# A graph-attention kernel: six PSUM banks a head that overlap the next head's, two matmuls for every i-tile, masks of -1

## What is computed

```python
seq = (x @ W_seq).reshape(N, H, DH)                  # N = 2048, H = 16, DH = 32
scores = leaky_relu(score1[:, :, None] + score2[:, None, :], 0.2)   # per head, (H, N, N)
attn = softmax(scores + (1 - adj) * -65500, axis=-1)
hidden = einsum('hij,jhd->ihd', attn, seq).reshape(N, 512)
x1 = layernorm(x + elu(hidden @ W_out + b_out))
A = D^-1/2 ((adj + adj.T) / 2 + I) D^-1/2            # second layer, same adj
out = layernorm(x1 + (adj @ A) @ x1)
```

## Time and profile before

| | us |
|---|---|
| median of 3 runs (lowest, highest) | 741.42 (740.29, 742.1) |
| profiled execution | 740.72 |
| its span, first to last instruction | 738.9 |

### The profile page before, as it was taken

One profiled execution on the slowest core, in us unless ns is written; L12 is line 12 of the kernel. 1 busy time (PEld: TensorE's weight loads), 2 busy tenths in 40 slices (PEclk: granted clock), 3 DMA queues, 4 the chain that ended last, 5 costly groups with the idle time before them and its releaser, 6 DMA issues.

```text
span 738.9 us, 23474 instructions
## 1 busy us (share of the span) xinstructions
PE 722.7 (98%) x10731; PEld 560.0 (76%) x10731; DVE 526.6 (71%) x885; ACT 409.6 (55%) x315; POOL 117.6 (16%) x145
## 2 busy tenths in 40 slices
PE   7999899999999999999999999999999999999996
PEld 5878899999999999999999995444444444444444
DVE  4568999999999999999999984877830110332332
ACT  1678998888988998898988952333220110000000
POOL 0200110001221212213000002655312100000000
PEclk9999999999999999999999999999999999999999
DMA  9994315213532344333221122994059500101101
GB/s 334 417 419 162 110 54 149 61 46 74 88 63 64 61 82 83 63 65 59 59 59 36 47 82 50 184 188 101 23 87 170 85 1 1 41 31 43 43 29 43
DMA packets 33351, 71.24 MB, mean 96 GB/s; under 512 B 3044, under 2 KB 14052, under 8 KB 31076
## 3 DMA queue, kind: packets, MB, share of 16 engines
q1 hardware_dynamic: 24736, 51.64, 20.3%
q0 software_dynamic: 8240, 17.84, 17.0%
q10 hardware_dynamic: 276, 0.26, 0.1%
HBM read 77.86 MB, written 8.65 MB: 117 GB/s over the span
## 4 chain that ended last, share of the span: by engine, by line
PE 81%; DVE 8%; issue 5%; DMA 4%; SPq 1%; POOL 1%; ACT 0%; POOLq 0%; DVEq 0%; ACTq 0%
PE bank L635 20%; PE bank L742 14%; PE bank L636 12%; PE bank L728 11%; PE bank L691 8%; PE bank L641 4%; PE bank L699 4%; PE bank L640 4%; PE bank L639 4%; DVE RZ L1081 3%; DMA RZ<-in_L_gnn_W_seq_dram 2%; DVE RG L1095 1%; DMA RZ<-s_rows_dram 1%; DVE RG L1091 1%; SPq L345 1%
## 5 line engine op out<-in xcount | busy, mean ns | idle before, releaser
L635 PE MATMUL bank<-RP,RG 128*128 128x132 f16 (+1 forms) x3072 | 375.3, 220 | 2.8 <-DVE RG L1091 1.5
L636 PE MATMUL bank<-RP,MT 128*128 128x66 f16 (+1 forms) x3072 | 375.0, 196 | 0.0
L820 ACT ACTIVATE RZ<-RZ,TAB 128x2048 int8<-128x2048 f32 x159 | 305.0, 1994 | 24.8 <-DVE RG L1091 22.1
L635 PEld LDWEIGHTS bank<-RP,RG 128*128 128x128 fp8e4 x3072 | 284.8, 98 | 3.7 <-DVE RG L1091 1.8
L636 PEld LDWEIGHTS bank<-RP,MT 128*128 128x128 fp8e4 x3072 | 284.7, 97 | 0.0
L640 PE MATMUL bank<-RP,RG 128*128 128x66 f16 (+1 forms) x1024 | 199.2, 194 | 0.0
L641 PE MATMUL bank<-RP,MT 128*128 128x66 f16 (+1 forms) x1024 | 198.9, 194 | 0.0
L639 PE MATMUL bank<-RP,RG 128*128 128x66 f16 (+1 forms) x1024 | 198.0, 193 | 0.0
L1081 DVE TENSOR_SCALAR RZ<-RZ,TAB 128x2048 int8<-128x2048 f32 x97 | 123.0, 1268 | 2.3 <-DMA RZ<-s_rows_dram 2.2
L742 PE MATMUL bank<-RZ,MT 128*128 128x512 f16 (+1 forms) x544 | 110.8, 366 | 0.0
L1091 DVE TENSOR_TENSOR RG<-RZ,MT 128x512 int32<-128x512 int32 x159 | 107.7, 677 | 0.0
(11 more groups left out here) (138 smaller groups left out, 724.1 us busy)
## 6 DMA issues: line engine op xcount, KB each, us to landing
RG<-in_adj_t_dram SPq DMA_DIRECT2D x16, 1024.0 KB, 8.1
RZ<-s_rows_dram SPq DMA_DIRECT2D x60, 256.0 KB, 3.3
seq_copy_dram<-SEQ SPq DMA_DIRECT2D x8, 528.0 KB, 5.4
RZ<-in_x_dram SPq DMA_DIRECT2D x16, 256.0 KB, 3.0
RP<-in_adj_p_dram POOLq DMA_DIRECT2D x8, 512.0 KB, 8.2
RP<-in_adj_tp_dram POOLq DMA_DIRECT2D x8, 512.0 KB, 12.4
out_dram<-W SPq DMA_DIRECT2D x16, 256.0 KB, 2.0
RQ<-in_x_t_dram SPq DMA_DIRECT2D x2, 1024.0 KB, 14.3
```

The costliest lines, as they stand in the source:

```text
L635: mm(bank[:, c:c + 4 * d], step, both, start=(j == 0 and i % IB == 0), **ends)
L636: last = mm(bank[:, c:c + 4 * d].rearrange("p (e c d) -> p e c d", e=2, c=2)[:, :, 1, :], mask, pn[:, 4:6, :], start=False, **ends)
L820: A(Z[:, m % NZ, :], S1B[u], ACT.Sign, bias=S2[:, h, j:j + 1], scale=-1.0).then_inc(z_ready, 1)
```

## The change

- A head now has six banks: four "front" banks with three i-tiles each (tiles 0 to 11) and two "back" banks with two tiles each (12 to 15). Head h starts at bank 6h mod 8, so two of its front banks are free of the head before, and the other four banks are those of that head's front.
- Every i-tile takes two matmuls, 132 and 66 columns (136 and 68 in head 2).
- Order on TensorE: for j = 0 to 3 of a head only tiles 0 to 5; then a wait on `front_free` of the head before; tiles 6 to 15 for j = 0 to 3; j = 4 to 11 whole; for j = 12 to 15 tiles 0 to 11 (then `front_ps`), and at last tiles 12 to 15 for these j. Head 0 does tiles 0 to 11 of j = 0 and 1 first.
- Eviction in two parts: ScalarE copies the fronts after its tile 9 and the backs after its tile 10; VectorE adds the fronts after its tile 8 and the backs after its tile 9; scaling moves to tile 10, norms to tile 11. In every fourth head the fronts are two stretches of banks and so two instructions.
- The mask is -1 in fp8, the step +127 in int8 (VectorE) or `Relu` with a scale of 2^40 in fp8 (ScalarE). The mask sum then has the opposite sign by itself: the negation at L1009 and the memset go, later additions become subtractions. A table `SK` with s2 times 2^40 is added.
- VectorE makes the steps of tiles (1, 4, 7, 10, 13) in odd heads, five in place of six.
- The output projection has its products in banks 0 and 1 and its transposes in banks 2 and 3 (the early ones of rows 0 and 1 in 0 and 1).

```diff
@@ constants
+    STEP = 127.0
+    STEEP = 2.0 ** 40
-    IB = 4
-    NB = NT // IB
+    NBH, WHOLE = 6, 12
-    OWNS = ((0, 1, 4, 6, 9, 12, 14),) + (OWN,) * (H - 1)
+    FIRST = [(WHOLE, 2)] + [(NT - WHOLE + 2, 4)] * (H - 1)
+    LAST = 12
+    OWN_B = (1, 4, 7, 10, 13)
+    OWNS = ((0, 1, 4, 6, 9, 12, 14),) + tuple(OWN_B if h % 2 else OWN for h in range(1, H))
@@ places of the sums
+        def place(h, i):
+            b, at = (i // 3, i % 3) if i < WHOLE else (WHOLE // 3 + (i - WHOLE) // 2, (i - WHOLE) % 2)
+            return (NBH * h + b) % 8, at
+
+        def fronts(h):
+            first = NBH * h % 8
+            return ((first, 2, 0), ((first + 2) % 8, 2, 6)) if first + 4 > 8 else ((first, 4, 0),)
+
+        def backs(h):
+            return (((NBH * h + 4) % 8, 2, WHOLE),)
@@ GpSimd, second_tables
+                own.mark(gp.tensor_scalar(SK[:, hs], S2[:, hs], STEEP, 1.0, ALU.mult, ALU.mult))
@@ TensorE, the loop over heads
                 if h >= 2:
-                    pe.wait_ge(banks_free, 2 * h - 2)
-                for j in range(NT):
+                    pe.wait_ge(back_free, BACK[h - 1])
+                def sums(j, tiles):
+                    s = (h * NT + j) % NG
+                    pn = operands(h)[:, j, :, :]
+                    both, edge = pn.rearrange("p c d -> p (c d)"), pn[:, 1:4:2, :]
+                    for i in tiles:
+                        b, at = place(h, i)
+                        c = at * 4 * d
+                        step, mask = G8[:, s, i * P:(i + 1) * P], MT8[:, j, i * P:(i + 1) * P]
+                        mm(pb[b][:, c:c + 4 * d], step, both, start=(j == 0 and at == 0), stop=(j == NT - 1), skip_group_check=True)
+                        last = mm(pb[b][:, c:c + 4 * d].rearrange("p (e c d) -> p e c d", e=2, c=2)[:, :, 1, :], mask, edge,
+                                  start=False, stop=(j == NT - 1), skip_group_check=True)
+                    return last
+
+                first, upto = FIRST[h]
+                for j in range(upto):
                     pe.wait_ge(g_ready, h * NT + (j + 1))
...
+                    sums(j, range(first))
+                if h == 0:
+                    pe.wait_ge(seq_sb, 2 * NT)
+                else:
+                    pe.wait_ge(front_free, FRONT[h])
+                for j in range(upto):
+                    sums(j, range(first, NT)).then_inc(g_used, 1)
+                for j in range(upto, LAST):
+                    pe.wait_ge(g_ready, h * NT + (j + 1))
+                    sums(j, range(NT)).then_inc(g_used, 1)
                     if h == 0:
                         second_half(j)
+                for j in range(LAST, NT):
+                    pe.wait_ge(g_ready, h * NT + (j + 1))
+                    last = sums(j, range(WHOLE))
+                last.then_inc(front_ps, 1)
+                for j in range(LAST, NT):
+                    sums(j, range(WHOLE, NT)).then_inc(g_used, 1)
@@ ScalarE
-                A(MT8[:, t, :], adj_f[:, t % NA, :], ACT.Copy, saturate=False, accum_out=CS[:, t:t + 1]).then_inc(adj_cast, 1)
+                A(MT8[:, t, :], adj_f[:, t % NA, :], ACT.Copy, scale=-1.0, saturate=False, accum_out=CS[:, t:t + 1]).then_inc(adj_cast, 1)
-                A(operands(h)[:, :, 0:5:4, 0:DV], V2[:, :, :, :], ACT.Copy).then_inc(hi_ready, 1)
+                A(operands(h)[:, :, 0:2, 0:DV], V2[:, :, :, :], ACT.Copy).then_inc(hi_ready, 1)
+            def front_lows(h):
+                sc.wait_ge(front_ps, h + 1)
+                if h >= 1:
+                    sc.wait_ge(hid_done, h)
+                low_sums(h, fronts(h), front_low)
+
+            def back_lows(h):
+                sc.wait_ge(g_used, NG + (h + 1) * NT)
...
-                A(Z[:, m % NZ, :], S1B[u], ACT.Sign, bias=S2[:, h, j:j + 1], scale=-1.0).then_inc(z_ready, 1)
+                A(Z8[:, m % NZ, :], S1B[u], ACT.Relu, bias=SK[:, h, j:j + 1], scale=STEEP, saturate=False).then_inc(z_ready, 1)
                     if j == AT_LOWS and h > 0:
-                        low_sums(h - 1)
+                        front_lows(h - 1)
+                    if j == AT_LOWS + 1 and h > 0:
+                        back_lows(h - 1)
@@ VectorE
-                own.mark(V.tensor_tensor(pn[:, :, 2:6:3, 0:DV], V2[:, :, :, :], pn[:, :, 0:5:4, 0:DV], ALU.subtract))
-                own.wait(ve)
-                V.tensor_scalar(pn[:, :, 1:4:2, 0:DV], pn[:, :, 4:6, 0:DV], -1.0, None, ALU.mult).then_inc(pn_ready, 1)
+                V.tensor_tensor(pn[:, :, 2:4, 0:DV], V2[:, :, :, :], pn[:, :, 0:2, 0:DV], ALU.subtract).then_inc(pn_ready, 1)
+            def front_sums(h):
+                ve.wait_ge(front_low, FRONT[h + 1])
+                whole_sums(h, fronts(h), front_free)
+
+            def back_sums(h):
+                ve.wait_ge(back_low, BACK[h + 1])
...
-                own.mark(V.scalar_tensor_tensor(ND, TN[:, :, 0, :], TINY, ND, ALU.add, ALU.add))
-                own.wait(ve)
-                own.mark(V.memset(TB[:, :, IB - 1, 0:DV], 0.0))
+                own.mark(V.scalar_tensor_tensor(ND, TN[:, :, 0, :], TINY, ND, ALU.add, ALU.subtract))
-                V.tensor_scalar(ZD[:, m % 2, :], S1B[u], S2[:, h, j:j + 1], -1.0, ALU.is_gt, ALU.mult).then_inc(zd_ready, 1)
+                V.tensor_scalar(ZD[:, m % 2, :], S1B[u], S2[:, h, j:j + 1], STEP, ALU.is_gt, ALU.mult).then_inc(zd_ready, 1)
                 if h > 0 and j == AT_EVAC + 1:
-                    whole_sums(h - 1)
+                    front_sums(h - 1)
                 if h > 0 and j == AT_EVAC + 2:
+                    back_sums(h - 1)
+                if h > 0 and j == AT_EVAC + 3:
                     scale_sums(h - 1)
                     add_sums(h - 1)
-                if h > 0 and j == AT_EVAC + 3:
+                if h > 0 and j == AT_EVAC + 4:
                     norms(h - 1)
```

More of the change, by code:

```diff
@@ L313, in gat_then_normalised_adjacency, with banks, of_tiles, turned @@
         DS = bass.ds
-        def wide(h, e):
-            d = DV + 1 if h == ROW_HEAD else DV
[L317 to L328, removed]
+        def place(h, i):
[6 more added lines that the diff above has]
+            return (((NBH * h + 4) % 8, 2, WHOLE),)
+        def banks(h, part, e):
+            d = DV + 1 if h == ROW_HEAD else DV
+            first, count, tile = part
+            k = 2 if tile == WHOLE else 3
+            return PS[:, first:first + count, 0:k * 4 * d].rearrange("p b (i e c) -> p b i e c", i=k, e=2)[:, :, :, e, :]
+        def of_tiles(m, part):
+            first, count, tile = part
+            k = 2 if tile == WHOLE else 3
+            return m[:, tile:tile + count * k, :].rearrange("p (b i) c -> p b i c", i=k)
+        copies = [2 if h == ROW_HEAD else 1 for h in range(H)]
+        FRONT = [sum(len(fronts(g)) * copies[g] for g in range(h)) for h in range(H + 1)]
+        BACK = [sum(copies[:h]) for h in range(H + 1)]
+        def turned(t, k):
+            return t if t < 2 and k < KC - 1 else 2 + t % 2
         def s1_row_there(engine, h):
@@ L621, in _ @@
                 if h >= 2:
-                    pe.wait_ge(banks_free, 2 * h - 2)
-                for j in range(NT):
+                    pe.wait_ge(back_free, BACK[h - 1])
+                d = DV + 1 if h == ROW_HEAD else DV
+                def sums(j, tiles):
                     s = (h * NT + j) % NG
-                    pe.wait_ge(g_ready, h * NT + (j + 1))
[L626 to L637, removed]
-                        else:
-                            mm(bank[:, c:c + 2 * d], step, high, start=False, **ends)
-                            mm(bank[:, c:c + 2 * d], step, low, start=False, **ends)
-                            last = mm(bank[:, c + d:c + 3 * d], mask, edge, start=False, **ends)
-                    last.then_inc(g_used, 1)
@@ new lines, in whole_sums @@
+            def whole_sums(h, parts, free):
+                c = DV if h == ROW_HEAD else 2 * DV
+                if h == ROW_HEAD:
+                    for part in parts:
+                        degrees(h, part)
+                for part in parts:
+                    for e in range(2 * DV // c):
+                        m = of_tiles(TB, part)[:, :, :, e * c:(e + 1) * c]
+                        V.tensor_tensor(m, m, banks(h, part, 0)[:, :, :, e * (c + 1):e * (c + 1) + c], ALU.add).then_inc(free, 1)
```

117 lines of the change are left out of this document (54 added, 63 removed).

## The result

The changed kernel takes 771.17 us (770.17 to 772.47) against 741.76 us for the one before in the same comparison: ratio 1.0398, with an interval of 1.0371 to 1.0426. It is 29 us slower, and outside the range of 737.5 to 751 us. Its profiled execution took 770.17 us, with a span of 768.4.

A forecast was written before the change was run, and what follows sets the result against it. TensorE's pace in the attention was taken as the bound. From 740.72 us profiled: start -0.6, stall +5.5, pairs -3.8, end -0.4 (together +0.6 after rounding), clock +1.9, profiled to median 0.7, giving 743.9 us; range 737.5 to 751.

The forecast's parts named there:

- What bounds the kernel: Attention, over half the span: TensorE sets the pace; VectorE is busy 97% of it, ScalarE 87%.
- Matmuls: Attention on TensorE: 1,024 matmuls fewer, one in nine, at 4.04 ns each beside their columns, 4.1 us gained.
- Relu: ScalarE's step as Relu into fp8: no extra cost, at most 0.1 us a step, and no second table load.
- the gap: Second matmul's moving operand, two runs of 33 values: taken as free; slow end 16.5 us, 760 us, chance 0.05.
- Start: Head 0: without L1009 all behind it comes 0.46 us earlier; with head 0's pairs, -0.6 us.
- The new wait of head 1: TensorE waits once on front_free at tile 6 of head 1, 96.4 to 101.9 us, a 5.5 us stall.
- The clock: After head 1's stall the granted clock falls, some 3.8 us at half the pace, costing 1.9 us.
- The later heads: Front evictions after head 1: 2.0 to 2.2 us against 3.6 us of TensorE work, so no stall.
- The sum: Whole kernel: profiled 740.72 us, +0.6, clock +1.9, and 0.7 from profiled to median, 743.9 us; chance 0.45.
- Rival 2: Slower, a stall in every head from ScalarE's load or eviction over 3.6 us; 7 us per 0.5 us, 751 us; chance 0.10.
- The end: Output projection behind the last head: the first products start 0.4 us sooner, 1.1 us after the last pair.

The follow-up runs named there:

- the early eviction: Changed kernel with two constants changed: VectorE sums fronts after tile 4 and ScalarE copies them after tile 5, ahead of its high copy; 729.34 us, ratio 0.9845.
- the run with filled stalls: Changed kernel with useless matmuls ahead of TensorE's wait on the front sums, 120 in head 1 and 48 in other odd heads; 763.21 us, ratio 1.0291.
- The third buffer: Changed kernel with three operand buffers in place of two, so ScalarE's high copy waits for an earlier head; 737.41 us, ratio 0.9949.
- the copy order: Changed kernel with two buffers, ScalarE's high copy after tile 10 behind its front and back copies, VectorE's low operands after tile 12; 737.34 us, ratio 0.9941.

## Why the prediction was wrong, point by point

- **What bounds the kernel**: right. TensorE's pace set the time before, and a gain in matmuls reaches the end when nothing else is in the way, as in the early eviction.
- **Matmuls**: right in sign, too small. Forecast 4.1 us by 4.04 ns for each of 1,024. A tile took 91.6 ns before (0.3664 / 4) and takes 88.8, 2.8 x 4,096 = 11.5 us. An extra matmul is 4.8 ns (measured), which explains 5 us of it; the other 6 us are pairs that went from 90.3 to 88.8 ns, where the prediction took for granted that they would keep their pace. The Trainium skill's 2.5 ns (TensorE: Matmul & The Clock Gate, "Wait — 56ns, not 53.3ns?") is below the averages measured here: 3.2 ns beside the columns of each matmul in pairs, 4.8 for one more.
- **Relu, the gap**: right, both cost nothing. A step is 1,994 ns as before. The trace has one table load, as before. The Trainium skill's ScalarE: Activation LUTs, "Table sets: the hidden batching unit", has relu in every set; the trace agrees, as Relu brought no second load.
- **Start**: near. Head 1's wait began at 95.83 us in place of 96.4. L1009 gave its 0.46 us; by luck the score row also came 0.39 us earlier in this trace, and the 200 pairs from there on were 0.4 us shorter.
- **The new wait of head 1**: right in place, cause and length, 5.72 us for 5.5, ended by VectorE's front sum at 101.55 us for 101.9.
- **The clock**: right that it falls in that stall, and near in price: low for 3.4 us, 3.0 of them with work to do, so 1.5 us for 1.9. The prediction had only a row with 4 us of idleness ahead of a low clock and looked at no shorter one; four of the five stalls of 2.7 us in the odd heads 5 to 13 had the low clock behind them too, and the run with filled stalls puts 10.4 us on all falls together.
- **"The later heads: no stall as long as both engines stand ready"**: this step failed. It added up the front copy, the sum and the signals, 2.0 to 2.2 us, and set them against 3.6 us. It did not list what else of ScalarE stands ahead of that copy and what that waits for; for head 1 it had counted the high copy and the step of tile 9, for the later heads neither. The chain is 4.4 us in even heads and 6.3 in odd ones. `high_operands` (L789 of the kernel before) has a wait on `g_used`, which never held anything up before, when ScalarE came to it with TensorE some 3 us into the next head: in the earlier trace rows it only waits for VectorE. The stall of head 1 itself changed that. It gave VectorE and ScalarE the lead that they need, and with this lead ScalarE reaches the wait before TensorE has ended the head. That the lead comes from the stall is read from the trace (the copy's wait of 4.13 us in head 2, right behind it); no run takes the stall away alone. The third buffer took away the wait and the copy order its place, and each time 33 us went.
- **The sum without this error**: with the high copy's wait out of the way the kernel takes 737.4 us, still 6.5 below the forecast of 743.9 and just under the stated range. So the failed step is not the whole error: the gain in matmuls was too small by 7 us in the other direction, and the stalls hid it.
- **Rival 2** had the right outcome, a stall in every head, and the wrong mechanism and price. It put the point at ScalarE's load (0.1 us more a step) with a price of 7 us for each half us. ScalarE was idle when it mattered. Its other condition, an eviction trip over 3.6 us, was met, but by a wait, a copy and a step that it did not count in the trip. The waits of heads 2 to 14 are 23.2 us, more than three times its price.
- **The end**: the early products begin 1.26 us behind the last pair in place of 1.50; 0.4 was forecast, 0.24 was got.
- **Accounting**: from the last wait in head 0 to the end of the attention it is 399.7 us (77.20 to 476.90) in place of 369.1 (78.07 to 447.20), 30.6 more. The 14 stalls are 28.9 us of idle time and 31.3 us of lost pace, since each is counted from the end of a matmul (0.20 us after its start) and not from the 0.03 us at which the next would have started; the clock is 10.4; 4,016 tiles at 2.8 ns less are -11.2; together 30.5. With 0.87 us of earlier start and 0.24 at the end this is 29.4 us of the 29.45 between the two profiled executions.

## What to carry to other kernels

When a change gives one engine a new wait, walk the full in-order list of each engine on the way to the signal, and for each instruction ahead of the one wanted write down what it waits for, also waits that the trace never shows: they were met only because of the old lead. A copy for which the bounding engine waits belongs ahead of one that waits for this engine. How far ahead an engine runs is a resource of its own: where an eviction stands in the lists decides it, and here two constants were worth 41 us.

## What the runs showed of the hardware

- The granted clock fell to its lower level behind stalls of 2.72 us (heads 7, 9, 11 and 13) and not behind one of the same length (head 5) nor any under 1 us; matmuls with no use in the same stalls kept it up and made the kernel 7.9 us faster, although 1.9 us of them filled no stall.
- Two matmuls of 132 and 66 columns took 88.8 ns here and 90.3 in the kernel before, from start to start. Columns written just ahead explain nothing of it; the operand's distance in memory and its gap changed the pair by 0.3 ns each (89.2 ns).
- Splitting a matmul of 132 columns into two of 66 cost 4.8 ns for each one added.
